# Two Swin blocks and iterative-norm whitening: the order of TensorE's products in the attention half, and a centring product in fp32 instead of two rounded parts

## What is computed

```python
def swin_block_fn(x, shift, mask, ...):
    y = layer_norm(x, ln1_g, ln1_b)
    if shift:
        y = jnp.roll(y, (-shift, -shift), axis=(1, 2))
    wins = y.reshape(Bn, Hh // WS, WS, Ww // WS, WS, Cc)
    wins = wins.transpose(0, 1, 3, 2, 4, 5).reshape(-1, N, Cc)
    qkv = (wins @ qkv_w + qkv_b).reshape(-1, N, 3, HEADS, hd).transpose(2, 0, 3, 1, 4)
    q, k, v = (qkv[0], qkv[1], qkv[2])
    attn = jnp.einsum('whnd,whmd->whnm', q, k) * hd ** (-0.5)
    attn = attn + bias[None]
    attn = attn.reshape(Bn, NW, HEADS, N, N) + mask[None, :, None]
    attn = jax.nn.softmax(attn.reshape(-1, HEADS, N, N), axis=-1)
    out = jnp.einsum('whnm,whmd->whnd', attn, v).transpose(0, 2, 1, 3).reshape(-1, N, Cc)
    out = out @ proj_w + proj_b
    ...
    x = x + out
    z = layer_norm(x, ln2_g, ln2_b)
    z = jax.nn.gelu(z @ fc1_w + fc1_b, approximate=False)
    return x + (z @ fc2_w + fc2_b)
```

## Time and profile before

| | |
|---|---|
| median of 3 runs | 780.66 us |
| the profiled execution | 782.55 us |
| its span, first to last instruction | 780.8 us |
| mean granted TensorE clock | 0.946 |
| TensorE busy | 693.6 us, 89% |
| VectorE busy | 534.0 us, 68% |
| ScalarE busy | 357.8 us, 46% |
| GpSimd busy | 205.0 us, 26% |
| chain that ended last | PE 36%, DVE 5%, issue 3%, ACT 2%, DMA 2% |

### The profile page before, as it was taken

The page is one execution under the profiler, slowest core; times in us unless marked ns, Lnnn a source line. Parts: engine busy times, 40 slices in busy tenths (PEclk is TensorE's granted clock), DMA queues, the critical chain, the costliest instruction groups (busy, mean ns, idle before and its releaser), DMA issues. The chain is left out here.

```text
span 780.8 us, 27044 instructions
## 1 busy us (share of the span) xinstructions
PE 693.6 (89%) x11574; PEld 414.3 (53%) x11574; DVE 534.0 (68%) x919; ACT 357.8 (46%) x628; POOL 205.0 (26%) x505
## 2 busy tenths in 40 slices
PE   3766999899999998899768999999999987999778
PEld 2633556556666655343334566666566553434557
DVE  1744797788888865787456898887798555782123
ACT  2512455445545544675434455455355444764200
POOL 4000022123222112346500231231122124797000
PEclk9866999999999999999978999999999998999859
DMA  9200121112112111000000121121121110000004
GB/s 228 46 21 21 36 65 55 54 57 68 59 58 69 56 58 38 23 1 1 21 21 25 57 74 54 58 75 52 53 68 61 58 39 23 2 1 1 2 21 144
DMA packets 47627, 37.56 MB, mean 48 GB/s; under 512 B 28564, under 2 KB 47124, under 8 KB 47508
## 3 DMA queue, kind: packets, MB, share of 16 engines
q1 hardware_dynamic: 46496, 33.96, 14.9%
q10 hardware_dynamic: 1012, 1.87, 0.8%
HBM read 18.15 MB, written 4.01 MB: 28 GB/s over the span
## 5 line engine op out<-in xcount | busy, mean ns | idle before, releaser
L423 POOL TENSOR_TENSOR att<-osb,rec 128x392 f32<-128x392 f32 x64 | 71.1, 1111 | 365.5 <-DMA rec<-dens 365.5
L812 DVE TENSOR_REDUCE nmax<-psum 113x16 f32<-113x784 f32 x128 | 117.6, 959 | 42.7 <-PE psum L1024 42.5
L532 ACT ACTIVATE pt<-psum 113x784 f32<-113x784 f32 x128 | 98.6, 824 | 90.5 <-PE psum L1024 90.5
L1024 PE MATMUL psum<-bt,rows_r 117*113 117x392 f32 x256 | 79.0, 409 | 3.9 <-DVE nmax L812 1.2
L838 DVE RECIPROCAL rpk<-dpk 64x49 f32<-64x49 f32 x64 | 28.9, 452 | 53.6 <-DMA dpk<-osb 53.1
L1024 PE MATMUL psum<-pt,vbd 113*32 113x49 f32 x4096 | 59.8, 209 | 3.8 <-ACT osb L539 3.6
L491 ACT ACTIVATE lv<-psum,epsc 128x392 f32<-128x392 f32 x32 | 18.8, 588 | 96.8 <-PE psum L1024 95.6
L416 POOL TENSOR_TENSOR xl<-XW,xh 128x392 fp32r<-128x392 f32 x24 | 31.9, 1329 | 108.3 <-ACT xh L499 108.3
L1024 PE MATMUL psum<-kexp,qsb 32*49 32x196 f32 x2048 | 59.8, 341 | 0.5 <-DMA kexp<-ksb 0.5
L1024 PEld LDWEIGHTS psum<-pt,vbd 113*32 113x32 f32 x4096 | 50.7, 110 | 15.6 <-issue 14.5
L383 POOL TENSOR_TENSOR XW<-XW,wcol 128x49 f32<-128x49 f32 (+5 forms) x200 | 55.3, 314 | 11.8 <-DVE XW L911 11.6
(11 more groups left out here) (174 smaller groups left out, 1221.9 us busy)
## 6 DMA issues: line engine op xcount, KB each, us to landing
rec<-dens SPq DMA_DIRECT2D x64, 196.0 KB
kexp<-ksb SPq DMA_DIRECT2D x128, 49.0 KB
qexp<-qsb SPq DMA_DIRECT2D x128, 49.0 KB
XW<-x_dram SPq DMA_DIRECT2D x14, 196.0 KB, 4.6
out_dram<-XW SPq DMA_DIRECT2D x14, 196.0 KB, 2.4
dpk<-osb SPq DMA_DIRECT2D x64, 12.2 KB
dens<-rpk SPq DMA_DIRECT2D x64, 12.2 KB, 2.6
pt<-w_dram ACTq DMA_DIRECT2D x2, 384.0 KB, 7.6
```

The costliest lines, as they stand in the source:

```text
L423: nc.gpsimd.tensor_tensor(att[:, 4 * part:4 * part + 4, :], osb[part][:, :].rearrange("p (a n) -> p a n", a=4), rec[part][:, :].rearrange( ...
L532: nc.scalar.activation(pt[grp][:, b:b + 2, :], SC[0:KROWS, b:b + 2, 0:BANK], ACT.Exp)\
L812: nc.vector.tensor_reduce(nmax[:, b:b + 2, grp, :], SC[0:KROWS, b:b + 2, 0:BANK].rearrange("p a (k m) -> p a k m", m=NTOK), AX.X, ALU.max, ...
L1024: return nc.tensor.matmul(o, a, b, start=start, stop=stop, **k)
```

## The change

- The third part of the pt buffer: exp of group 0 alternates between two, so exp need not wait for pv of the half before.
- In a step TensorE does pv of **both** groups of half G-1 together (group 0 into bank bB, group 1 into bO), where before pv of group 0 of half G stood at the end of step G, and that of group 1 at the start of the next. ScalarE's two osb copies come together after the first exp.
- wv moves behind `scores` of group 0, next to proj. proj goes to bO.
- Centring, k and variance stand together before bt of group 1. q stands alone after fold_r, at the step's end, and goes to bO.
- Centring is one fp32 product for all halves; `x_high`, `x_low`, xh, xl are gone.
- VectorE takes the row maxima of group 0 before both reciprocals. SyncE issues both gathers, both stores and both reads in pairs.
- At the end of a phase pv of half 15 stands around the MLP's first variance and spread products.

The diff, cut to these parts; the residuals read bO accordingly, and ScalarE reads q from bO from half 2 on:

```diff
@@ -150,7 +149,11 @@
...
 rx = sb("rx", [128, 2 * GWIN, NTOK], F32R)
-pt = [ptb[0:KROWS, i] for i in range(2)]
+pt = [ptb[0:KROWS, i] for i in range(3)]
+
+def pt_of(g, grp):
+    return pt[1 if grp else 2 * (g % 2)]
+
@@ -324,16 +325,17 @@
...
             if G > base:
-                gather(G - 1, 1)
-                to_rows(G - 1, 0)
-                from_rows(G - 1, 0)
-                to_rows(G - 1, 1)
-                from_rows(G - 1, 1)
+                for part in range(2):
+                    gather(G - 1, part)
+                for part in range(2):
+                    to_rows(G - 1, part)
+                for part in range(2):
+                    from_rows(G - 1, part)
             if G + 2 < base + HALVES:
...
                 spread_q(G + 2)
-            gather(G, 0)
         G = base + HALVES - 1
+        gather(G, 0)
         to_rows(G, 0)
@@ -409,13 +411,6 @@
...
-    def x_low(blk, g):
-
-        pool.wait_ge(xh_done, NSPLIT * blk + g)
-        pool.wait_ge(xc_ready, HALVES * blk + g + AHEAD)
-        nc.gpsimd.tensor_tensor(xl[:, :], xcols(blk, g + AHEAD), xh[:, :].bitcast(F32), ALU.subtract)\
-            .then_inc(xl_done, 1)
-
@@ -524,47 +509,45 @@
...
-    def expo(g, grp, first=False):
+    def expo(g, grp):
         act.wait_ge(st_ready, 2 * g + grp + 1)
-        if not first:
-            act.wait_ge(av_ready, 2 * (g - 1) + grp + 1)
+        if grp and g:
+            act.wait_ge(av_ready, 2 * g)
+        elif g > 1:
+            act.wait_ge(av_ready, 2 * g - 3)
         for b in (0, 2):
-            nc.scalar.activation(pt[grp][:, b:b + 2, :], SC[0:KROWS, b:b + 2, 0:BANK], ACT.Exp)\
+            nc.scalar.activation(pt_of(g, grp)[:, b:b + 2, :], SC[0:KROWS, b:b + 2, 0:BANK], ACT.Exp)\
                 .then_inc(exp_done, 1)
-    def o_copy(g, part, first=False):
+    def o_copy(g, part, bank):
         act.wait_ge(av_ready, 2 * g + part + 1)
-        if not first:
+        if g:
             act.wait_ge(att_done, 2 * (g - 1) + part + 1)
-        nc.scalar.activation(osb[part][:, :], bO[:, 0:4 * NROWS], ACT.Copy).then_inc(osb_done, 1)
+        nc.scalar.activation(osb[part][:, :], bank[:, 0:4 * NROWS], ACT.Copy).then_inc(osb_done, 1)
...
         f = first and base == 0
-        expo(G, 0, f)
+        expo(G, 0)
         if first:
...
         else:
-            o_copy(G - 1, 1, base == 0 and g == 1)
+            o_copy(G - 1, 0, bB)
+            o_copy(G - 1, 1, bO)
         if ahead > 0:
...
             square(G + 3)
-            variance(G + 3, 1 - u)
         if ahead > 1:
             evac_k(p, G + 2, f)
+        if ahead > 2:
+            variance(G + 3, 1 - u)
+        expo(G, 1)
+        if ahead > 1:
             evac_q(p, G + 2, u, (G + 1) // 2 + 1)
-        if g + 1 + AHEAD < HALVES:
-            x_high(base // HALVES, g + 1)
-        if tail and ahead > 0:
-            tail[1]()
-        expo(G, 1, f)
-        o_copy(G, 0, f)
-        if tail and ahead == 0:
-            tail[1]()
@@ -848,10 +833,10 @@
...
         else:
-            recip(G - 1, 0, blk == 0 and g == 1)
             if ahead > 0:
                 rowmax(G + 1, 0)
-            recip(G - 1, 1, blk == 0 and g == 1)
+            for part in range(2):
+                recip(G - 1, part, G == 1)
         if g > 1:
@@ -1027,23 +1012,19 @@
...
-    def f_xc_split(blk, g):
-
-        pe.wait_ge(xl_done, NSPLIT * blk + g)
-        mm(bX[:, 0:TOK], centre_r[:, :], xh[:, :], True, False)
-        mm(bX[:, 0:TOK], centre_r[:, :], xl[:, :], False, True).then_inc(xc_ready, 1)
-
...
-    def f_qk(p, g1, buf, free=None):
+    def f_k(p, g1, buf):
...
         mm(bA[:, 0:TOK], p["wk"][:, :], z[buf][:, :]).then_inc(k_ready, 1)
-        pe.wait_ge(*(free or (rx_done, g1)))
-        mm(bB[:, 0:TOK], p["wq"][:, :], z[buf][:, :]).then_inc(q_ready, 1)
+
+    def f_q(p, buf, bank):
+
+        mm(bank[:, 0:TOK], p["wq"][:, :], z[buf][:, :]).then_inc(q_ready, 1)
@@ -1098,36 +1079,35 @@
...
-    def pv(g, grp, buf, first=False):
+    def pv(g, grp, buf, bank):
...
             pe.wait_ge(v_done, 2 * g + 2)
-        if not first:
-            pe.wait_ge(osb_done, 2 * g + grp)
         for win in range(GWIN):
...
                     c0 = (2 * win + hg) * NTOK
-                    last = mm(bO[32 * h4:32 * h4 + 32, c0:c0 + NTOK],
+                    last = mm(bank[32 * h4:32 * h4 + 32, c0:c0 + NTOK],
                               vbd[buf][:, (GWIN * grp + win) * HEADS + 4 * hg + h4, :],
-                              pt[grp][:, h4, c0:c0 + NTOK])
+                              pt_of(g, grp)[:, h4, c0:c0 + NTOK])
         last.then_inc(av_ready, 1)
-    def proj(p, g, bank=bA):
+    def proj(p, g):
...
                 for w in range(2):
-                    last = mm(bank[64 * w:64 * w + 64, 0:TOK].rearrange("p (x i n) -> p x i n", i=2, n=NTOK)[:, :, i],
+                    last = mm(bO[64 * w:64 * w + 64, 0:TOK].rearrange("p (x i n) -> p x i n", i=2, n=NTOK)[:, :, i],
                               p["wph"][:, hh, 64 * i:64 * i + 64], att[:, w::2, hh * NTOK:(hh + 1) * NTOK],
...
-        G = HALVES * blk + g
+        base = HALVES * blk
+        G = base + g
         first = g == 0
@@ -1135,48 +1115,57 @@
...
         else:
-            pv(G - 1, 1, nb)
+            pv(G - 1, 0, nb, bB)
+            if ahead > 0:
+                pe.wait_ge(q_done, G + 2)
+            else:
+                pe.wait_ge(res_done, G - 2)
+            pv(G - 1, 1, nb, bO)
         if ahead > 0:
+            scores(p, blk, nb, G + 1, 0, lambda i: (exp_done, 4 * G + 1 + i))
             pe.wait_ge(k_done, G + 2)
             f_v(p, nb)
-            scores(p, blk, nb, G + 1, 0, lambda i: (exp_done, 4 * G + 1 + i))
-        if ahead > 2:
-            pe.wait_ge(z_done, G + 3)
-            if first:
-                if blk:
-                    pe.wait_ge(relay_done, AHEAD // 2 + 1)
-                f_xc(blk, G + AHEAD)
-            else:
-                f_xc_split(blk, g)
         if tail:
...
         if g > 1:
-            if ahead > 0:
-                pe.wait_ge(v_done, 2 * G + 4)
+            pe.wait_ge(osb_done, 2 * G)
             proj(p, G - 2)
...
         if ahead > 2:
+            pe.wait_ge(z_done, G + 3)
+            if blk:
+                pe.wait_ge(relay_done, (g + AHEAD) // 2 + 1)
+            f_xc(blk, G + AHEAD)
+        if ahead > 1:
+            pe.wait_ge(v_done, 2 * G + 4)
+            f_k(p, G + 2, u)
+        if ahead > 2:
             if first:
                 pe.wait_ge(var_used, G + 3)
+            else:
+                pe.wait_ge(osb_done, 2 * G - 1)
             f_var(G + 3)
...
             tail[1]()
-        if ahead > 1:
-            if g > 1:
-                pe.wait_ge(res_done, G - 1)
-            else:
-                pe.wait_ge(v_done, 2 * G + 4)
-            f_qk(p, G + 2, u, (var_used, G + 4) if ahead > 2 else (rx_done, G + 1))
         scores_t(p, blk, u, G, 1, u, pair,
...
         if ahead > 0:
-            if ahead > 1:
-                pe.wait_ge(q_done, G + 3)
+            if ahead > 2:
+                pe.wait_ge(var_used, G + 4)
+            elif ahead > 1:
+                pe.wait_ge(osb_done, 2 * G - 1)
             maxt(G + 1)
-        pv(G, 0, u, first and blk == 0)
+        if ahead > 1:
+            if g > 1:
+                pe.wait_ge(res_done, G - 1)
+            elif g:
+                pe.wait_ge(osb_done, 2 * G)
+            elif blk:
+                pe.wait_ge(mres_done, base)
+            f_q(p, u, bO)
@@ -1336,28 +1328,40 @@
...
+        def xc_first():
+            pe.wait_ge(osb_done, 2 * G - 3)
+            m_xc(0)
+
         def var_first():
-            pe.wait_ge(res_done, G - 2)
+            pe.wait_ge(v_done, 2 * G + 2)
             m_var(0)
...
         def xc_second():
+            pe.wait_ge(osb_done, 2 * G - 1)
             m_xc(1)
-            pe.wait_ge(mvar_used, pairs + 1)
...
         def var_second():
-            pe.wait_ge(res_done, G - 1)
+            pe.wait_ge(mvar_used, pairs + 1)
             m_var(1)
-        step(p, blk, HALVES - 2, 0, 1, pair=PAIRS - 1, tail=[lambda: m_xc(0), var_first, copied])
-        step(p, blk, HALVES - 1, 1, 0, pair=PAIRS - 1, tail=[xc_second, spread_first, var_second])
-        pv(G, 1, 1)
+        def nothing():
+            pass
+
+        step(p, blk, HALVES - 2, 0, 1, pair=PAIRS - 1, tail=[xc_first, var_first, copied])
+        step(p, blk, HALVES - 1, 1, 0, pair=PAIRS - 1, tail=[xc_second, nothing, nothing])
+        pe.wait_ge(res_done, G - 1)
+        pv(G, 0, 1, bO)
+        var_second()
+        spread_first()
+        pe.wait_ge(osb_done, 2 * G + 1)
+        pv(G, 1, 1, bO)
         m_xc(2)
```

47 lines of the change are left out of this document (21 added, 26 removed).

## The result

The changed kernel takes **803.08 us** (median of 4 runs, 800.51 to 807.09) where the kernel before took 780.79 beside it (4 runs, 780.63 to 787.19): ratio **1.0261, 95% interval 1.0208 to 1.0314**. Forecast was 770.8. It is slower, and outside the range. The profiled execution took 804.04 with a span of 802.3, 21.5 more than before's 780.8; its mean clock, 0.952, is no lower than before's 0.946.

What follows compares the result with a forecast made beforehand. TensorE, busy 97% of the steady halves, was taken as the bound. Steady halves -7.7, first halves -6.6, half 1 -0.4, half 13 -0.4, half 14 +0.6, ends +4.6 sum to -9.9: from 780.66 to 770.8 us, range 763 to 781.

Steps and rivals of the forecast that it cites:

- 14.6 a half, so 22 x (14.95 - 14.60) = -7.7: Halves 2 to 12 of both blocks: most of the 8.6 us lost in disturbed halves goes, saving 7.7 us.
- -0.04 against 14.56, so 14.52: Undisturbed steady half: sum of removed and added TensorE work, form changes and waits, taking 14.56 us to 14.52.
- pv comes in (+0.66): Steady half outside ScalarE's window: a pv group moves in there and adds 0.66 us of TensorE time.
- Rival 2: Before sel_r: back-to-back GpSimd products slow VectorE's links, rx comes late; 780.7 to 790.6 us; chance 0.14 slower, 0.08 no change.
- The window fold_r to sel_r: Steady half, fold_r to next sel_r: ScalarE's two exponentials set it, so it stays 2.31 us despite two fewer form changes.
- Rival 1: Steady halves: every removed form change pays, the exponentials' window being no limit; halves of 14.1, 762 us; chance 0.14.
- The centring product, +0.33: Steady half: one fp32 centring product streams 0.66 us where the xh, xl pair streamed 0.33, so +0.33 on TensorE.
- The first halves, -3.3 each: First half of each block: bn and kexp go ahead of the wait for z, saving 3.3 us each, 6.6 in all.
- of the two cases the slower: First half, after the wait for z: slow clock stays, -2.2 us; the other case keeps 2.4 GHz, -4.9.
- Halves 13 and 14: Late halves of both blocks: half 13 saves 0.4 us; half 14, with pv added and wv parted from proj, costs 0.6.
- The ends, +2.3 each: After half 15 of each block: osb copies and the softmax-sum chain end later, costing 2.3 us a block, 4.6 in all.
- The drain between tile forms: TensorE in a steady half: each change of form costs 0.19 us; two fewer outside ScalarE's window save 0.38.

Runs made afterwards that it cites:

- a_rx3_pv98: Changed kernel with rx after the third VectorE link instead of the fourth, and 49-column pv pairs made single 98-column products (half the value weights dropped): 771.70 us, ratio 0.9814.
- b_dve: Kernel before with only VectorE's row maxima of group 0 ahead of its reciprocal and SyncE's two stores ahead of both reads: 772.96 us, ratio 0.9771.
- a_pv98: Changed kernel with each pair of 49-column pv products made one of 98, half the value weights left out: 777.61 us, ratio 0.9887 to before.

## Why the prediction was wrong

- **"14.6 a half, so 22 x (14.95 - 14.60) = -7.7"** is the step that failed; it came out at +16.4. The steady half itself was nearly right: -0.04 against 14.56, so 14.52; 14.67 stands in the trace of after, 14.57 to 14.60 in 21 of the 22 halves of a_rx3_pv98. Right too was that the disturbances of the earlier trace rows go; b_dve shows that, with 321.7. What failed is the silence on what comes in their place. I costed each group at its duration in the old order, "pv comes in (+0.66)", as if it did not matter which groups stand beside it. Beside each other, pv, pv and kexp ask for instructions faster than they come: 16.5 to 17.4 us. This term was put at nothing, no rival held it, and the rows to doubt it by were there: pv's 49-column products have the most instructions per column, and the change puts 128 of their records in a row. The trace of the kernel before even has a small stop of the kind, in a pv group with qexp before it (PEld; 2.5 us after an instruction transfer started):

```profile
224.44 0.16 PEld L1024 LDWEIGHTS psum<-pt,vbd 113*32 113x32 f32 x8 [0.30 <-issue]
224.89 0.70 PEld L1024 LDWEIGHTS psum<-pt,vbd 113*32 113x32 f32 x56 [0.29 <-issue]
```

- **Rival 2** (VectorE, rx late) happened, at its place and by its mechanism, in half of the halves. "With two (2 x 0.7) rx is 0.4 late"; measured 0.65 to 0.81, on 11 of 22 halves, and 6.3 to 7.2 us in the steady sum. It was given 0.14 as the whole story for slower; alone (a_pv98 still has it) it leaves the kernel faster than before. So it was neither the cause of the sign nor negligible.
- **The window fold_r to sel_r**, "2.31": 2.32. Rival 1 did not happen: with both causes gone the half stays at 14.57 to 14.60 and not 14.1. In the undisturbed half above, the loads for bt wait 0.64 and 0.45 for pt, where the kernel before has the 0.42 of the earlier trace rows.
- **The centring product, +0.33**: confirmed alone in the old order (14.56 became 14.85 to 14.89).
- **The first halves, -3.3 each**: -2.5 and -2.4. bn and kexp went ahead of the wait for z as reckoned, and of the two cases the slower held: the clock over the stretch is 0.74 in block 0 and 0.79 in block 1, and the products behind the wait run slow (from centring to k 1.46 in block 0 and 1.44 in block 1, where an undisturbed half has 0.76):

```profile
76.00 0.57 DVE L792 TENSOR_TENSOR z<-psum,ly 128x392 f32<-128x392 f32 x1
...
76.62 1.67 PE L1009 MATMUL psum<-XW,conb 128*128 128x392 f32 x2 [2.21 <-DVE z L792]
78.08 1.51 PE L1009 MATMUL psum<-z,wk 128*128 128x392 f32 x2
```

- **Halves 13 and 14**: +2.4 and +1.1 for -0.4 and +0.6. In a_rx3_pv98 they are 14.77, 14.05 and 15.04, 15.02. So half 14's own term was right within 0.1 a block, and half 13's excess of 1.1 and 1.0 goes with the same two edits.
- **The ends, +2.3 each**: +3.9 and +0.8. That their sum is right is luck in part: the two ends were priced alike. The latency was right: "about 11.5" from pv's start to the end of the first GpSimd product, measured 661.53 + 1.01 - 650.99 = 11.55, and TensorE's last pv waits 2.92 for it instead of 1.82.

```profile
650.99 1.64 PE L1009 MATMUL psum<-pt,vbd 113*32 113x49 f32 x128
...
661.53 1.01 POOL L418 TENSOR_TENSOR att<-osb,rec 128x392 f32<-128x392 f32 x1 [11.74 <-DMA rec<-dens]
...
663.18 1.54 PE L1009 MATMUL psum<-pt,vbd 113*32 113x49 f32 x64 [2.92 <-ACT osb L526]
```

- **The drain between tile forms**: the Trainium skill, TensorEngine Tiling (Array Packing), Key Properties, says that changing the tiling mode drains the engine. The pieces agree, at somewhat less than the 0.19 of the prediction: pv, pv without a change in between take 1.57 to 1.66 and two single groups 2 x 0.85, so 0.04 to 0.13; wv and proj beside each other take 0.91 + 1.43 and apart 1.01 + 1.48, so 0.15. Together that is 0.19 to 0.28 where the forecast took 0.38, and the half came out 0.05 to 0.08 above 14.52. The saving is small against what the dense neighbours cost in supply.

## What to carry to other kernels

Count instructions as well as columns. Grouping products of one form saved up to 0.15 us a change here, but if they are small it also makes the densest run of instructions. The sign that instructions are missing was idle time in the middle of a group with "issue" as its releaser. Before a large reorder, try its small parts on the old order: here one swapped pair of lines on each of VectorE's and SyncE's queues gave 2.3% [1.5%, 3.1%], more than was forecast for the whole change (1.3%).
